# Grouped attention: the causal mask and the scale move from TensorE and ScalarE to VectorE, the exponentials go head by head with their sums

## The reference, cut to what matters

```
NH, KVH, HD = 32, 4, 128
q = _rope((h @ Wq).reshape(B, S, NH, HD), pos)
k = _rope((h @ Wk).reshape(B, S, KVH, HD), pos)
v = (h @ Wv).reshape(B, S, KVH, HD)
k, v = jnp.repeat(k, NH // KVH, axis=2), jnp.repeat(v, NH // KVH, axis=2)
scores = jnp.einsum('bqhd,bkhd->bhqk', q, k) / jnp.sqrt(jnp.float32(HD))
causal = jnp.tril(jnp.ones((S, S), dtype=bool))
scores = jnp.where(causal[None, None], scores, jnp.float32(-1000000000.0))
attn = jax.nn.softmax(scores, axis=-1)
o = jnp.einsum('bhqk,bkhd->bqhd', attn, v).reshape(B, S, NH * HD) @ Wo
x = resid + o
```

## Time and profile before

| | |
|---|---|
| median of 3 runs | 1608.36 us (1606.78 to 1617.46) |
| profiled execution | 1605.54 us, its span 1603.8 us |
| TensorE busy | 1484.3 us, 93% |
| VectorE busy | 908.2 us, 57% |
| GpSimd busy | 782.3 us, 49% |
| ScalarE busy | 614.4 us, 38% |
| TensorE's granted clock, mean | 0.931 |

### The profile page before, as it was taken

How to read it: one execution, slowest core, us unless ns; L and a number is a source line. 1 busy time by engine, 2 the same in 40 slices (tenths; PEclk the granted TensorE clock), 3 DMA queues, 4 the chain that set the end, 5 groups by cost and what they waited for, 6 DMA issues and landing times. The chain is left out here.

```text
span 1603.8 us, 20759 instructions
## 1 busy us (share of the span) xinstructions
PE 1484.3 (93%) x7316; PEld 1112.9 (69%) x7316; DVE 908.2 (57%) x1597; ACT 614.4 (38%) x1101; POOL 782.3 (49%) x605
## 2 busy tenths in 40 slices
PE   6898999899987999999999998978999998799998
PEld 4686466544444766766666665557988877699998
DVE  1653111235657686776777753567878773445454
ACT  2332121123332344344343443356666653233333
POOL 1850102025563797798888864057465541233332
PEclk7886999579997999999999999889999997799999
DMA  8004111440001110110110000200110001334441
GB/s 298 1 1 145 47 44 42 134 127 23 24 0 38 56 57 1 56 57 1 56 57 1 19 2 1 81 27 3 51 53 2 27 1 40 104 121 120 120 120 51
DMA packets 60317, 88.61 MB, mean 55 GB/s; under 512 B 7556, under 2 KB 44612, under 8 KB 60230
## 3 DMA queue, kind: packets, MB, share of 16 engines
q1 hardware_dynamic: 59206, 85.82, 16.7%
q0 software_dynamic: 1024, 1.64, 0.4%
HBM read 81.92 MB, written 5.41 MB: 54 GB/s over the span
## 5 line engine op out<-in xcount | busy, mean ns | idle before, releaser
L960 ACT ACTIVATE prob<-PS 121x800 f32<-121x800 f32 x192 | 157.9, 838 | 247.7 <-PE PS L1934 244.8
L1343 DVE TENSOR_REDUCE mx<-PS 128x1 f32<-128x482 f32 (+1 forms) x312 | 185.7, 650 | 42.2 <-PE PS L1914 41.3
L619 POOL TENSOR_TENSOR e_wl<-e_wf,e_wh 128x768 fp32r<-128x768 f32 x33 | 70.8, 2146 | 184.3 <-ACT e_wh L884 159.7
L696 POOL TENSOR_TENSOR hT<-hT,prob 121x800 f32<-121x800 f32 x56 | 109.0, 1947 | 66.6 <-ACT prob L960 64.7
L1913 PE MATMUL PS<-kth,qs 128*128 128x482 f32 (+1 forms) x312 | 128.3, 411 | 13.5 <-DVE kl L1336 5.8
L1949 PE MATMUL PS<-prob,kvn 121*64 121x400 f32 (+1 forms) x768 | 136.1, 503 | 0.9 <-ACT prob L960 0.9
L696 POOL TENSOR_TENSOR xc<-xc,prob 121x800 f32<-121x800 f32 x56 | 117.6, 2100 | 12.3 <-ACT prob L960 6.8
L1914 PE MATMUL PS<-kl,qm 66*128 66x482 f32 (+1 forms) x312 | 122.1, 391 | 0.0
L1931 PE MATMUL PS<-qs,kth 128*121 128x400 f32 (+1 forms) x384 | 110.9, 371 | 8.0 <-DMA qm<-nml 4.7
L1934 PE MATMUL PS<-qm,kl 66*121 66x400 f32 (+1 forms) x384 | 103.4, 351 | 0.0
L1949 PEld LDWEIGHTS PS<-prob,kvn 121*64 121x64 f32 (+1 forms) x768 | 52.3, 137 | 71.2 <-issue 68.9
(11 more groups left out here) (278 smaller groups left out, 3596.7 us busy)
## 6 DMA issues: line engine op xcount, KB each, us to landing
e_wb<-routing SPq DMA_DIRECT2D x32, 400.0 KB, 4.0
wgu<-in_L_ffn_gate_up_proj SPq DMA_DIRECT2D x8, 1024.0 KB, 13.8
krt<-in_ctx_T SPq DMA_DIRECT2D x8, 722.0 KB, 4.1
ksw<-in_ctx_Tswap SPq DMA_DIRECT2D x8, 722.0 KB, 5.7
wdn<-in_L_ffn_down_proj SPq DMA_DIRECT2D x8, 512.0 KB, 7.9
wq<-in_L_ffn_Wq SPq DMA_DIRECT2D x4, 1024.0 KB, 5.2
wo<-in_L_ffn_Wo SPq DMA_DIRECT2D x4, 1024.0 KB, 5.6
e_wf<-in_L_ffn_Wg SPq DMA_DIRECT2D x32, 128.0 KB, 2.2
```

The lines of the kernel that those rows point to most:

```text
L619: pool.tensor_tensor(m["wl"][:, slot], m["wf"][:, slot], m["wh"][:, slot].bitcast(fp32), ALU.subtract).then_inc(ms["wlo"], 1)
L696: pool.tensor_tensor(acc, acc, prob[:, n % RING], ALU.add).then_inc(xb["ap"], 1)
L960: act.activation(prob[0:k, n % RING], PS[0:k, 2 * (n % 2):2 * (n % 2) + 2, 0:GC], ACT.Exp).then_inc(xb["ex"], 1)
L1343: dve.tensor_reduce(mx3[:, m, g:g + 1], PS[:, 4 + k % 3, 0:SEG[g][1]], AX.X, ALU.max).then_inc(xb["free"], 1)
```

## The change

VectorE now multiplies the scores by the scale and adds the mask, in one operation from PSUM into d2; then it takes the negated row maxima from d2. ScalarE takes the exponential of each head (100 columns) with that negated maximum as bias and sums it into su2 on the way. TensorE's mask product, VectorE's row sums and the wait between sum and reciprocal go. exps2 waits for the maxima (at["mx"]) in place of the subtraction (at["sub"]); at["sub"] now tells TensorE that the bank is free after the first operation. nmx2 has three buffers in place of two.

```diff
-        mx2 = sb("mx2", [S, 2, 4], stack=st2)
+        nmx2 = sb("nmx2", [S, 3, 4], stack=st2)
...
             def exps2(v):
-                act.wait_ge(at["sub"], U0 + v + 1)
-                act.activation(d2[:, v % 3], d2[:, v % 3], ACT.Exp, scale=SCALE1).then_inc(at["exp"], 1)
+                act.wait_ge(at["mx"], U0 + v + 1)
+                for j in range(4):
+                    last = act.activation(d2[:, v % 3, j], d2[:, v % 3, j], ACT.Exp, bias=nmx2[:, v % 3, j:j + 1],
+                                          accum_out=su2[:, v % 3, j:j + 1])
+                last.then_inc(at["exp"], 1)
...
                 dve.wait_ge(at["s"], U0 + v + 1)
-                dve.tensor_reduce(mx2[:, v % 2], bank, AX.X, ALU.max).then_inc(at["mx"], 1)
-                dve.wait_ge(at["mx"], U0 + v + 1)
                 if v >= 3:
                     dve.wait_ge(at["norm"], U0 + v - 2)
-                dve.tensor_tensor(d2[:, v % 3], bank, mx2[:, v % 2, :, None].to_broadcast([S, 4, S]),
-                                  ALU.subtract).then_inc(at["sub"], 1)
+                dve.scalar_tensor_tensor(d2[:, v % 3], bank, SCALE1, causal[:, None, :].to_broadcast([S, 4, S]),
+                                         ALU.mult, ALU.add).then_inc(at["sub"], 1)
+                dve.wait_ge(at["sub"], U0 + v + 1)
+                dve.tensor_reduce(nmx2[:, v % 3], d2[:, v % 3], AX.X, ALU.max, negate=True).then_inc(at["mx"], 1)
 
             def inverse_sum2(v):
 
                 dve.wait_ge(at["exp"], U0 + v + 1)
-                dve.tensor_reduce(su2[:, v % 3], d2[:, v % 3], AX.X, ALU.add).then_inc(at["sum"], 1)
-                dve.wait_ge(at["sum"], U0 + v + 1)
                 dve.reciprocal(sm2[:, v % 3], su2[:, v % 3]).then_inc(at["rec"], 1)
...
                 if v >= 2:
                     pe.wait_ge(at["sub"], U0 + v - 1)
-                mm(PS[0:S, v % 2, 0:4 * S].rearrange("p (h s) -> p h s", s=S), identb[0:S, 0:S],
-                   causal[:, None, :].to_broadcast([S, 4, S]), start=True, stop=False)
                 for j in range(4):
                     last_ = mm(PS[0:S, v % 2, j * S:(j + 1) * S], q2[:, (HG * x + 4 * k + j) % QRING, b % HB * S:(b % HB + 1) * S],
-                               kr[:, x // 2, toks(b)], start=False, stop=(j == 3))
+                               kr[:, x // 2, toks(b)], start=True, stop=True)
                 last_.then_inc(at["s"], 1)
```

## The result

The changed kernel takes 1651.2 us in the median of four runs (1643.4 to 1655.4), the kernel before 1607.6 beside it: a ratio of 1.029, with a 95% interval of 1.025 to 1.033. The forecast was 1657 us. The profiled executions, 1652.97 and 1605.54, differ by 47.4 us.

What follows compares the result with a forecast made beforehand. The circle of VectorE and ScalarE was to bound the stage at 3.23 + 1.80 = 5.03 us a unit: units 0 to 57 take 300.6 against 248.1 (+52.5), less 1.2, +51.3 on 1605.5 gives 1657 us; range 1626 to 1690.

Steps and rivals of the forecast that it cites:

- The circle: VectorE and ScalarE waiting for each other in each second-layer attention unit: 3.80 us becomes 5.03, over TensorE's 3.94.
- fixed part: All of the circle between two maxima except the exponential: 3.23 us a unit, taken as unchanged.
- TensorE's wait ahead of the values: New TensorE wait in each unit, put down to VectorE's low halves (o2l): about 1.1 us, clock at 1.00.
- Four exponentials: ScalarE's one exponential a unit cut into four with pointer bias: 1.24 us without sums, 1.80 with them.
- The fetch: ScalarE instruction fetching each exponential's sum: 0.14 us each, between 0.09 overlapped and a four-head upper end of 2.52.
- free sums: Rival: the accumulating exponentials on ScalarE need no fetch, so the four take 1.24 and the time is 1628; chance 0.16.
- The long units: Six units where TensorE waits for low output weights, plus unit 4: 5.64 less the mask's 0.17, 5.47 us each.
- rival of the falling clock: Rival: idle TensorE is granted 1.2 GHz, its unit 7.9 us; 1802 if all 51 units, 1693 if a quarter; chance 0.05.
- The end: Open units from 58 on, no queries left to rotate: with the start, each saves a mask, 7 × 0.17 = 1.2 us.
- The mask product: TensorE's mask matmul ahead of the scores, removed: 0.17 us a unit, paying only while TensorE is the limit.
- VectorE's sum: VectorE's removed row sum, 0.559 us a unit, 35.8 in all, priced at nothing because VectorE then waits for swaps.

Runs made afterwards that it cites:

- swaps-first kernel: The changed kernel with ScalarE's half swaps of the queries of s + 6 put ahead of the four exponentials of s: 1592.4 us, ratio 0.989.
- sums back: The changed kernel with the row sums taken by VectorE's reduction again and no accumulation on ScalarE: 1641.9 us, ratio 1.023, ordinary unit 4.44 us.
- kernel before, split in four: The kernel before the change with only its exponential cut into four of 100 columns, no pointer and no sum on ScalarE: 1620.5 us, ratio 1.009.

## Why the prediction was right, point by point

- *The circle is the limit once it is longer than TensorE's unit.* Right. Its fixed part measured 3.24 against 3.23, and taking the swaps out of it removed the whole price. That is shown, by the swaps-first kernel. TensorE's wait ahead of the values, put at about 1.1 us a unit, came out at 0.79 in 47 units.
- *Four exponentials.* Split, pointer and overlap were priced at 1.24 without sums; sums back gave 4.44 − 3.24 = 1.20. The pointer costs 0.09: an exponential of 100 columns took 366 ns with it and 275 in the kernel before, split in four. The estimate of 1.19 by the formula of the Trainium skill, "ScalarE: Activation LUTs", "What ACT_TABLE_LOAD costs", came nearer than my rows, and its 93 ns for a pointer operand agree with the 0.09 here.
- *The fetch*, 0.14 each, was the term that was mis-sized. It costs 0.095 on the path: 188 ns long, overlapped on both sides as exponentials in a row are. The row of one column with the full overlap, 0.09, which I had named as the lower price, was right and I leaned away from it. Four exponentials are therefore 1.58, not 1.80, and 51 units × 0.21 are 10.7 us less than forecast. The page of the Trainium skill that I named beside the free sums, "ScalarE activation tables: per-element evaluation and per-set limits", "What a function is on this engine", says that the cost does not depend on which table is read, with the same operands. It does not compare an activation with a sum to one without, so it says nothing for or against that rival.
- *The long units* were put at 5.47 for seven. Unit 4 was ordinary (4.85). The six measured 36.3 us together, 6.05 each. Their own chain was nearly right. In unit 10 the output matmuls start 2.61 us after the first operation and the next unit 3.11 after them, against 2.34 and, less the mask, 3.13. The low weights follow GpSimd's sum of the rotated queries by as much as before: 2.49 us from the start of that sum to TensorE's matmul in unit 10 then, 2.45 now (timeline of before, then after):

```profile
1100.56 1.06 POOL L717 TENSOR_TENSOR q<-q,qt 128x400 f32<-128x400 f32 x1 [0.69 <-DVE qt L1475]
1110.10 1.03 POOL L717 TENSOR_TENSOR q<-q,qt 128x400 f32<-128x400 f32 x1 [1.60 <-DVE qt L1478]
```

But before the change the maximum of unit 10 had waited 0.23 for TensorE and so stood nearer to them; now the first operation waits for nothing. TensorE's wait for the weights, 1.25 and now 2.56, grew because TensorE comes earlier, and is not itself the price. In the other two, units 26 and 42, TensorE's clock fell behind the wait, 4.55 in place of 3.11 in unit 26, which I had priced only as a rival. With unit 4 counted, the long units took back 2.9 us of the 10.7. The rival of the falling clock was thus right in two long units, though it set no ordinary one.
- *The end*, where I took off a mask a unit, came out 0.7 us longer than before: each unit behind unit 58 saved its mask (3.80 in place of 3.98), but TensorE waits 2.99 for the weights in unit 58, and its clock fell there too (6.19 us in place of 4.75, with 0.72 granted in place of 1.00).
- *The mask product* and *VectorE's sum* at nothing: right. Put back, each left the ordinary unit or the path as it was.
- Sum for units 0 to 57: forecast 300.6, measured 292.9 (1061.68 to 1354.61), before 248.1. Of the forecast's +51.3 us, 7.7 too many lie here; the end gave back 1.9, and the first unit started 2.1 later than in the profile of before, which no term of the sum holds. That the profiled execution came out at +47.4 is therefore in part luck, while the unit's length, 4.82 against 5.03, is not.

## What to carry to other kernels

Look for circles: two engines that each wait for the other within one unit have a length that no busy share shows. Once the circle is the longest, an instruction added to it lengthens every unit by what it takes from start to start, here 0.095 us for a fetch of 0.188, however idle both engines look. The cure here was the order within a queue: the same instructions behind the step that others wait for, not ahead of it, turned 1.029 into 0.989. And a sum taken "on the way" by an activation is an instruction in the queue, four of them here, so it pays only where the engine that it relieves is the one that ends last. Here VectorE was not, and taking the sum from it gained nothing.

## What the runs showed of the hardware

- An accumulating activation of 100 columns is two entries in the trace, ACTIVATE of 369 ns and ACTIVATION_READ_ACCUMULATOR of 188; in a row the pair takes 0.37 from start to start.
- A scalar_tensor_tensor with an immediate scalar and a bf16 operand took 568 ns for 400 columns from PSUM, 60 less than the one with its scalar in memory, whose other operand was fp32. No run here tells the two differences apart.
- The same wait of TensorE, 2.56 us, was followed by a lower clock in two of six units (0.67 granted over 4.6 us) and by none in the other four. In the kernel with the sums back a shorter wait, 2.18 to 2.19, was followed by it in all six, while the one at the end of that kernel, 2.61, was not. The length of the wait alone does not decide; why one wait brings it and another does not is left open.
